# A fourth key tile for VectorE in six odd heads, and a bias operand on ScalarE's exponentials

## The reference

```
query = heads(ct_q @ Wu_q) + heads(rope(ct_q @ Wq_r))      # ct_q = x @ Wd_q, all with biases
key   = heads(ct_kv @ Wu_k) + heads(rope(x @ Wk_r))        # ct_kv = x @ Wd_kv
value = heads(ct_kv @ Wu_v)
attn  = softmax(query . key / scale)                        # 16 heads, 4096 x 4096 each
x = layernorm(x + (attn . value) @ Wo + Wo_b)
x = layernorm(x + int8_ffn(x))                              # 256 x 256 weights, one scale for x
```

## Time and profile before

| | us |
|---|---|
| median of 3 runs | 1926.04 (1925.49 to 1926.55) |
| the profiled execution's own time | 1926.29 |
| its span, first to last instruction | 1924.5 |
| ScalarE busy in the span | 1802.0 (94%) |
| TensorE busy | 1849.6 (96%) |
| VectorE busy | 1580.2 (82%) |
| the exponentials: first start to last start | 126.2 to 1841.0 |

### The profile page before, as it was taken

One profiled execution on the slowest core, in us unless ns is written; L12 is line 12 of the kernel. 1 busy time (PEld: TensorE's weight loads), 2 busy tenths in 40 slices (PEclk: granted clock), 3 DMA queues, 4 the chain that ended last, 5 costly groups with the idle time before them and its releaser, 6 DMA issues.

```text
span 1924.5 us, 31443 instructions
## 1 busy us (share of the span) xinstructions
PE 1849.6 (96%) x12996; PEld 449.9 (23%) x12996; DVE 1580.2 (82%) x1499; ACT 1802.0 (94%) x2022; POOL 173.7 (9%) x132
## 2 busy tenths in 40 slices
PE   8989999999999999999999999999999999999975
PEld 3432222122222222222222222222222222222234
DVE  4858888888888888888888888888889888988467
ACT  3479999999999999999999999999999999999946
POOL 5735400000000000000000000000000000500010
PEclk9989999999999999999999999999999999999987
DMA  4453111111110111111121001111121101111002
GB/s 142 153 172 116 18 21 26 26 26 26 26 26 20 18 18 22 26 26 26 25 70 26 22 17 18 22 26 25 26 48 26 26 19 19 18 23 26 1 24 88
DMA packets 161367, 73.41 MB, mean 38 GB/s; under 512 B 129952, under 2 KB 146592, under 8 KB 160736
## 3 DMA queue, kind: packets, MB, share of 16 engines
q1 hardware_dynamic: 158272, 66.85, 15.0%
q10 hardware_dynamic: 2944, 4.47, 0.8%
HBM read 49.13 MB, written 20.84 MB: 36 GB/s over the span
## 4 chain that ended last, share of the span: by engine, by line
ACT 54%; PE 31%; issue 9%; DVE 4%; DMA 1%; POOL 0%; SPq 0%; ACTq 0%; DVEq 0%; POOLq 0%
ACT arena L901 54%; PE PS L704 15%; PE PS L655 9%; PE PS L1179 4%; PE PS L744 1%; DVE arena L961 1%; PE PS L1328 1%; DMA arena<-tables_dram 1%; DVE bn L832 1%; DVE arena L937 0%; DMA w<-weights_dram 0%; DVE absmax L1771 0%; DVE arena L1805 0%; DVE arena L824 0%; ACT arena L864 0%
## 5 line engine op out<-in xcount | busy, mean ns | idle before, releaser
L901 ACT ACTIVATE arena<-PS 128x1024 f32<-128x1024 f32 x1860 | 1707.8, 1325 | 8.3 <-PE PS L655 5.0
L704 PE MATMUL PS<-arena,Vh 128*32 128x512 f32 x8192 | 1092.6, 606 | 4.1 <-DVE arena L961 4.1
L655 PE MATMUL PS<-Qst,Kst 49*128 49x512 f16 x4096 | 724.0, 384 | 24.5 <-ACT arena L901 4.3
L961 DVE SCALAR_TENSOR_TENSOR arena<-arena 128x2048 f32<-128x2048 f32 x282 | 646.0, 2291 | 0.1
L937 DVE TENSOR_SCALAR arena<-PS 128x512 int32<-128x512 f32 x376 | 259.4, 690 | 247.1 <-PE PS L655 243.3
L655 PEld LDWEIGHTS PS<-Qst,Kst 49*128 49x128 f16 x4096 | 187.7, 93 | 1039.3 <-ACT arena L901 1008.8
L704 PEld LDWEIGHTS PS<-arena,Vh 128*32 128x32 f32 x8192 | 161.3, 108 | 317.5 <-issue 302.5
L957 DVE SCALAR_TENSOR_TENSOR arena<-arena 128x2048 f32<-128x2048 f32 x94 | 216.4, 2302 | 0.0
L945 DVE TENSOR_SCALAR arena<-arena 128x2048 int32<-128x2048 int32 x94 | 116.2, 1236 | 8.5 <-DVE arena L961 0.5
L947 DVE TENSOR_SCALAR arena<-arena 128x2048 int32<-128x2048 int32 x94 | 116.8, 1242 | 0.0
L1496 POOL TENSOR_SCALAR nmr<-mv 128x16 f32<-128x16 f32 x1 | 0.3, 262 | 1256.7 <-DVE mv L1660 1256.7
(11 more groups left out here) (118 smaller groups left out, 480.1 us busy)
## 6 DMA issues: line engine op xcount, KB each, us to landing
Kst<-k_halves SPq DMA_DIRECT2D x64, 128.0 KB
Qst<-q_halves SPq DMA_DIRECT2D x64, 128.0 KB
Vh<-head_values SPq DMA_DIRECT2D x30, 256.0 KB, 5.5
k_halves<-parts_or_sums SPq DMA_DIRECT2D x16, 256.0 KB, 2.9
q_halves<-parts_or_sums SPq DMA_DIRECT2D x16, 256.0 KB, 2.8
Kst<-k_halves SPq DMA_DIRECT2D x64, 64.0 KB
Qst<-q_halves SPq DMA_DIRECT2D x64, 64.0 KB
head_values<-arena SPq DMA_DIRECT2D x1, 4096.0 KB, 16.4
```

Source lines behind the costliest of these rows:

```text
L655: return nc.tensor.matmul(out, Kst[par][low:low + HK + 1, at:at + 128], Qst[par][low:low + HK + 1, j * CH:(j + 1) * CH], start=True, stop= ...
L704: last = nc.tensor.matmul(bank(value_bank(t))[32 * j:32 * j + 32, :], Vh[t % 2][:, kt, :], moving, start=kt == first, stop=kt == last_kt)
L901: nc.scalar.activation(ring(at, k), bank(g % SLOTS * SLOT, k), ACT.Exp, scale=EXP_SCALE).then_inc(a.exp, 1)
L961: last = nc.vector.scalar_tensor_tensor(out=t, in0=t, scalar=POLY[3 - j], in1=power if j == 3 else mantissa, op0=ALU.add, op1=ALU.mult)
```

## The change

In the heads 3, 7, 11, 15, 27 and 31 (`FOUR`) VectorE takes tile 14 as well. All odd heads share one SBUF buffer for their values, so tile 14's value rows and ones are scaled by V_SCALE in every odd head (`scaled`). In the ten odd heads that are not in `FOUR`, where ScalarE still makes tile 14, its exponential is made larger by 1 / V_SCALE through a bias: `small[:, 9:10]` holds -ln V_SCALE, `small[:, 8:9]` holds 0. In the code the bias is an operand of ScalarE's one exponential instruction, at every step of every head; where it isn't needed it points to the zeros. Without a bias argument, as before, the instruction has the number 0 there.

The blocks for VectorE become 13 in the time of heads 1 to 15 and 24 to 30, 12 in that of heads 16 to 23, and 4 in the last head's; URGENT goes from 4 to 8. The value rows of tile 14 are evacuated in two instructions (even and odd heads) where there was one. GpSimd sets one more column of ones. The slow path for extreme inputs, which doesn't run here, is adapted, and its loop has two heads to a turn.

```
+FOURTH, FOUR = 14, (3, 7, 11, 15, 27, 31)
 def by_vector(t):
-    return BY_VECTOR if t else FIRST_BY_VECTOR
+    return (FOURTH, *BY_VECTOR) if t in FOUR else BY_VECTOR if t else FIRST_BY_VECTOR
+def scaled(par):
+    return (FOURTH, *BY_VECTOR) if par else BY_VECTOR
 def head_blocks(t):
...
+    if FOURTH in low and t % 2:
+        low = [kt for kt in low if kt != FOURTH] + [FOURTH]
...
-URGENT = 4
+URGENT = 8
...
+BLOCKS_OF = [FIRST_BLOCKS] + [13 if t < 16 or t >= 24 else 12 for t in range(1, NT - 1)]
+BLOCKS_OF.append(QB * CYCLES - sum(BLOCKS_OF))
 def make_block_steps():
...
-        n = FIRST_BLOCKS if t == 0 else len(BY_VECTOR) * QB
-        n = min(n, QB * CYCLES - len(steps))
+        n = BLOCKS_OF[t]
...
-COPY_AFTER = {FIRST_BLOCKS - 1 + len(BY_VECTOR) * QB * t: t for t in range(NT - 1)}
+COPY_AFTER = {sum(BLOCKS_OF[:t + 1]) - 1: t for t in range(NT - 1)}
...
 def attention_scalar(act, a):
...
-                nc.scalar.activation(ring(at, k), bank(g % SLOTS * SLOT, k),
-                                     ACT.Exp, scale=EXP_SCALE).then_inc(a.exp, 1)
+                fourth = t % 2 == 1 and blocks[0][0] == FOURTH
+                nc.scalar.activation(ring(at, k), bank(g % SLOTS * SLOT, k), ACT.Exp, scale=EXP_SCALE,
+                                     bias=small[:, 8 + fourth:9 + fourth]).then_inc(a.exp, 1)
...
 def evacuate(p):
...
+                        given = PS[:, b * CH + k * D:b * CH + (k + 1) * D].rearrange("p (h r) -> p h r", r=HD)
+                        scales = [V_SCALE if kt in scaled(par) else 1.0 for par in range(2)]
+                        if scales[0] == scales[1]:
+                            last = nc.scalar.activation(V[:, :, kt, :], given, ACT.Copy, scale=scales[0])
+                        else:
+                            for par in range(2):
+                                last = nc.scalar.activation(V[:, par:H:2, kt, :], given[:, par:H:2, :], ACT.Copy, scale=scales[par])
...
 # GpSimd
-                for kt in by_vector(p):
+                for kt in scaled(1) if p else by_vector(0):
                     nc.gpsimd.memset(Vh[p][:, kt, HD:2 * HD], V_SCALE).then_inc(s_ones, 1)
```

More of the change, by code:

```diff
@@ L594, in build @@
         assert NOT_FIRST == list(range(KT - len(NOT_FIRST), KT))
-        ONES_ALL = 3 + len(by_vector(0)) + len(by_vector(1)) + 1
+        ONES_ALL = 3 + len(by_vector(0)) + len(scaled(1)) + 1
         def load_values(sp, s, t, par):
@@ L766, in serial_attention_tensor, with one_head @@
         def serial_attention_tensor(pe, a):
-            with pe.Fori(0, NT) as t:
+            def one_head(t, par):
                 pe.wait_ge(a.stack[0], 7 * 16 * (t + 1))
@@ L781, in serial_attention_tensor @@
                         last = nc.tensor.matmul(PS[32 * j:32 * j + 32, OT * CH:(OT + 1) * CH],
-                                                Vh[0][:, kt, :], P3[:, j * CH:(j + 1) * CH],
+                                                Vh[par][:, kt, :], P3[:, j * CH:(j + 1) * CH],
                                                 start=kt == 0, stop=kt == KT - 1)
                     last.then_inc(a.pv, 1)
+            with pe.Fori(0, NT // 2) as i:
+                for par in range(2):
+                    one_head(2 * i + par, par)
         def serial_attention_scalar(act, a):
[L787 to L793, removed]
+            with act.Fori(0, NT // 2) as i:
+                for par in range(2):
+                    for kt in range(KT):
+                        at = KT * (2 * i + par) + kt
+                        act.wait_ge(a.qk, QK0 + at + 1)
+                        act.wait_ge(a.pv, PV0 + at)
+                        less = kt in scaled(par)
+                        nc.scalar.activation(P3, bank(0, QB), ACT.Exp, scale=EXP_SCALE,
+                                             bias=small[:, 8 + less:9 + less]).then_inc(a.exp, 1)
         def serial_attention_vector(dve, a):
@@ L806, in one @@
                 sp.wait_ge(a.pv, PV0 + KT * t)
-                load_values(sp, a.vh[0], t, 0)
+                load_values(sp, a.vh[0], t, par)
                 store_head(sp, a, t, t, par)
@@ L1354, in evacuate @@
                         kt = 2 * e + k
-                        last = nc.scalar.activation(
-                            V[:, :, kt, :], PS[:, b * CH + k * D:b * CH + (k + 1) * D].rearrange("p (h r) -> p h r", r=HD),
-                            ACT.Copy, scale=V_SCALE if kt in BY_VECTOR else 1.0)
+                        given = PS[:, b * CH + k * D:b * CH + (k + 1) * D].rearrange("p (h r) -> p h r", r=HD)
[3 more added lines that the diff above has]
+                        else:
+                            for par in range(2):
+                                last = nc.scalar.activation(V[:, par:H:2, kt, :], given[:, par:H:2, :], ACT.Copy, scale=scales[par])
                     last.then_inc(s_ev, 1)
```

## The result

The changed kernel takes 2075.07 us, median of 4 runs (2073.46 to 2076.88), against 1925.76 for the kernel before on the same chip (1924.53 to 1926.55). The ratio is 1.0777, 95% interval 1.0764 to 1.0789. The forecast was 2072 with a range of 2050 to 2108.

What follows compares the result with a forecast made beforehand. ScalarE's exponentials were taken to set the pace, at 0.918 us each. The terms +160.8 (operand), -11.0 (steps), -5.0 (stops) and +0.9 (end) sum to +145.7 on 1926.04: 2072 us, range 2050 to 2108.

Steps and rivals of the forecast that it cites:

- The steps: Attention: six heads lose tile 14, so 12 of 1860 exponential steps are gone, 11.0 us less.
- The bias operand: ScalarE's exponentials: all 1848 now read a bias from SBUF, at 0.087 us each, +160.8 us.
- (a): Operand price from ScalarE's L1376, one bias, PSUM to SBUF, 512 wide: 0.575 - 0.493 = 0.082 us.
- (b): Operand price from ScalarE's L864, bias and scale from SBUF, 256 wide: 0.211 us with SBUF input, at most 0.105 per operand.
- (c): Operand price from ScalarE's L1431, one bias, SBUF input, 1024 wide: operand and SBUF input together cost 0.122 us.
- the rival of the dear operand: ScalarE's exponentials: all of 0.122 us is the operand's, +225.5 us, 2136 us in all; chance 0.07.
- The rival with the hidden operand: ScalarE's exponentials: the operand's fetch hides under their overlap, pace stays 0.918 us; about 1921 us in all; chance 0.10.
- Stops of ScalarE: Attention: of 8.3 us idle before exponentials, much heals at the slower pace since VectorE has spare time; -5.0 us.
- the rival in which TensorE loses its clock: Attention: more waiting per step lowers TensorE's granted clock, so value products would bound; 2200 us and more; chance 0.03.
- URGENT: Order of value products: 8 lets those of VectorE tiles come later; priced 0, since VectorE has 7 us to spare.
- The end: Last head: three value products stand behind the last exponential in place of two, +0.9 us.
- What would show it: Trace signs: exponentials about 1.005 us apart, `small` among inputs, ScalarE idle 2 to 4 us, VectorE's waits some 60 longer.

Runs made afterwards that it cites:

- e2: The kernel before, with a bias operand pointing to zeros on all 1860 exponentials and nothing else changed: 2081.86 us, ratio 1.0804.
- e1: The changed kernel, with the bias operand given only to the 20 exponentials that need it, none on the other 1828: 1932.69 us, ratio 1.0037.
- e4: As e1, with URGENT back at 4 in place of 8: 1932.62 us, ratio 1.0031.
- e5: The kernel before with URGENT 8 in place of 4 and nothing else of the change: 1921.05 us, ratio 0.9978.
- e7: The changed kernel with the bias operand in the odd heads' exponentials alone, 916 of 1848: 1998.18 us, ratio 1.0377.

## Why the prediction was right

*What bounds the kernel* held. ScalarE's exponentials set the pace and went on doing so. Every experiment is an account of their pace and their stops. The total was not right by luck: no large errors cancel. The three terms that were off, operand +1.8, stops +2.3 and what lies outside the attention some +0.7, all point the same way.

*The steps* held: 1848 exponentials, 11.0 us less.

*The bias operand* held in kind and size. Forecast 0.087 us, which no row of the kernel before shows and which was worked out from three other instructions; the change shows 0.088 (1.006 - 0.918), e2 0.087. Of the three ways to the price, (a), from the same path PSUM to SBUF with one bias, gave 0.082, and solving (b) and (c) together gave 0.089, so both were within 0.006. So of the 0.122 in (c), the end that the rival of the dear operand took, some 0.034 was not the operand's, if it costs as much there. The Trainium skill ("ScalarE: Activation LUTs", What ACT_TABLE_LOAD costs) gives about 93 ns for a pointer operand; this kernel shows 87 to 88 in 1848 and 1860 instructions, so by the page the changed kernel would be some 9 us slower than it is; the measurement decides.

*The rival with the hidden operand* fell by e2: the overlap of recorded durations, larger still with the operand, holds no room. Its number would have failed too. I put its kernel at about 1921, and e1, which is that case but for 20 operands (1.8 us), took 1932.7: I had counted the busy time of a head against its length, and added 3 to 4 us of stops in head 28 to a swap of head 3 for head 4. ScalarE stops for 20.7 us instead: 3.9 in head 28, about what I had, but also 5.1 in heads 3 and 4 (3.2 before), some 7 in heads 17 to 23 (some 3 before) and 3.6 in heads 0 and 1 (1.8 before). A block must be read at its own place in the order, since TensorE's next scores wait for that read; spare time later in the head does not pay for being late at one block.

*Stops of ScalarE*: the term that was mis-sized. Forecast -5.0, measured -2.7. I said that VectorE has over 7 us to spare in each head at the new pace. In a common head that is so (columns as in the earlier trace rows; VectorE is the third busy time):

```profile
471.00:529.00 58.00, 54.27 (x385) 10.96 (x384) 48.57 (x40) 58.00 (x60) 0.00 (x0) 1.00 0.12 21
```

48.57 us of 58.00, against a forecast of 49.2. The granted clock is 1.00 here and 0.987 over the whole execution, as it was before, so the rival in which TensorE loses its clock fell as well. (Its argument passed over the 0.92 in the first window of the earlier trace rows.) The spare time is not there in head 28 of the changed kernel (the stretch around it; then GpSimd; VectorE; TensorE; ScalarE):

```profile
1736.00:1795.00 59.00, 53.92 (x379) 10.72 (x382) 55.13 (x44) 56.56 (x58) 19.64 (x16) 0.97 0.11 21
...
1755.03 19.64 POOL L899 TENSOR_TENSOR ctkv<-arena,rows 128x256 f32<-128x256 f32 x16 [163.91 <-DVE arena L880]
...
1769.20 0.69 DVE L949 SCALAR_TENSOR_TENSOR sums_ok<-parts_or_sums,sums_ok 128x16 f32<-128x16 f32 x1
...
1771.23 2.85 DVE L983 SCALAR_TENSOR_TENSOR arena<-arena 128x2048 f32<-128x2048 f32 x1
1774.01 2.27 DVE L890 TENSOR_REDUCE absmax<-arena 128x1 f32<-128x2048 f32 x1
1776.21 0.67 DVE L959 TENSOR_SCALAR arena<-PS 128x512 int32<-128x512 f32 x1
...
1776.94 0.54 PE L669 MATMUL PS<-Qst,Kst 49*128 49x512 f16 x1 [1.96 <-DVE arena L959]
...
1779.98 3.12 ACT L923 ACTIVATE arena<-PS,small 128x1024 f32<-128x1024 f32 x3 [2.44 <-PE PS L669]
```

VectorE is busy 55.13 of 59.00 us. The rival with the hidden operand had this head at 54.9, which leaves 3.4 of 58.3, so "over 7 us to spare in each head" went against my own number. Polynomials that take longer while GpSimd adds, the normalisation (its instruction at 1769.20 is one row of it) and a reduction of 2.27 us come one behind another, the read at 1776.21 is late, and ScalarE stops for 2.44, though the head as a whole has time left. This is the stop that I had priced for the hidden operand only. Some 1.5 us stay in head 4 as well.

*URGENT* at 0: e4 against e1 shows 0 with 20 operands, though not for the reason given, since there the waits left are for reads; with all 1848 it was not tried. In the kernel before it is worth 4.5 us (e5).

*The end* held: +0.9 forecast, 2.98 - 2.04 = +0.9 measured up to the copy. The 0.7 behind the copy was not in the sum, nor 0.3 ahead of the attention, which I had named as the price without cover; neither is shown to be the change's.

*What would show it* came as written: starts 1.0055 apart for about 1.005, `small` among the inputs, VectorE's waits 61.9 us longer for about 60; only the idle is 5.6 for 2 to 4.

## What to carry to other kernels

Before an operand is added to an instruction that sets the pace, multiply its price by all instructions that will carry it, not by those that need it: the cure here was one line, an operand for 20 instead of 1848. Read that price from first to last start over a long run of such instructions, less its stops, and not from recorded durations or from two neighbouring starts. When work goes to an engine with slack, check the slack at each read that another engine waits for, not as a sum over a stage: in e1 the twelve steps saved (11.0 us) were lost to late reads.

## What the runs showed of the hardware

The operand costs 0.087 to 0.088 us in each of 1848 or 1860 exponentials back to back, and mixed into plain ones the pace follows it head by head (e7). While GpSimd's additions in SBUF run, many of VectorE's instructions that read SBUF take longer: a step of the polynomial up to 2.85 us in place of 2.28, above. One of the shortest takes 0.69 us at 1769.20, above, and with GpSimd at rest (from e1):

```profile
357.24 0.17 DVE L949 SCALAR_TENSOR_TENSOR sums_ok<-parts_or_sums,sums_ok 128x16 f32<-128x16 f32 x1
```

What is added is nearly the same here, 0.52 us for an instruction of 0.17 and 0.57 for one of 2.28. So it looks like one wait for each instruction, not like slower work all through it; what sets the wait was not tried. VectorE's block reads, whose input lies in PSUM, keep their 0.69 us.

In e1 a stand of TensorE is followed by its lower clock level: behind 2.60 us the granted clock of the stretch is 0.94, and eight matmuls take 1.93 us instead of 1.07.
